# Gate logits with the gate as the stationary operand, shorter fills and a new plan in a fused expert, attention and expert layer

## The chip, the cores and the metric

The kernel runs on one core of a Trainium2 chip. The metric is the device time of one execution in microseconds. A core has TensorE (PE, with its weight loads listed as PEld), VectorE (DVE), ScalarE (ACT), GpSimd (POOL) and SyncE (SP, which issues most DMAs). TensorE reads SBUF and writes PSUM, which has eight banks of 128 partitions by 512 fp32 values. TensorE's clock is granted at one of two levels, 1.2 or 2.4 GHz; the profile gives the mean of a stretch as a share of the higher.

## What is computed

The input is 16 sequences of 512 tokens of width 128, in fp32. Three sublayers follow one another, called A, B and C in the kernel:

```python
x = x + 0.5 * ffn(layernorm(x), gate_w, gate_b, w1, b1, w2, b2)   # A
x = x + attn(layernorm(x), Wq, Wkv_down, Wk_up, Wv_up, Wo)        # B: 8 heads of 32
x = x + 0.5 * ffn(layernorm(x), gate_w, gate_b, w1, b1, w2, b2)   # C

def ffn(x, gate_w, gate_b, w1, b1, w2, b2):      # 8 experts, top 2, hidden 256
    logits = einsum('bsd,ed->bse', x, gate_w) + gate_b
    probs = softmax(logits)
    topk_vals, topk_idx = top_k(probs, 2)
    h = relu(einsum('bsd,edh->bseh', x, w1) + b1)
    expert_out = einsum('bseh,eho->bseo', h, w2) + b2
    return sum over the two chosen experts of expert_out * topk_vals
```

## The kernel before

**Tiling and stages.** A batch is one sequence: four tiles of 128 tokens. Stage B works on single batches. Stages A and C group batches into chunks (A: 1, 1, 2, 3, 3, 3, 3 batches; C: 3, 3, 3, 3, 2, 1, 1). One chunk of each stage, the first of A and the last of C, is dense: all experts for all tokens (`dh`, `dy`). The others are routed: GpSimd scatters normalized rows into expert order in DRAM with indirect DMAs (`scat`, L1091), the rows come back in quads of up to four tiles of 128 rows of one expert each (`xload`, `xg`), TensorE runs both expert layers (`h`, `y`) with weights fetched per tile (`wload`), results go to DRAM, and GpSimd gathers two rows for each token (`gat`, L1111) that VectorE combines (`comb`).

**Routing.** For each batch and each of A and C, GpSimd scales the rows (`scaled`, L1126), TensorE transposes them (`xTf`, L1674), ScalarE copies them to `xT_F` (L1256), and TensorE forms the gate logits (`logits`): four matmuls with the 128 tokens of a tile as stationary side and the gate's 8 columns as moving side, so that the tokens lie on PSUM's partitions. VectorE adds the gate bias (L1396), and once the chunk's batches are there runs the top-2 choice (`top1`, `top2`) and the ranks (`rank1`, `rank2`). The rank tables `same_expert` and `spread` (L1050 to L1054) are made by GpSimd at the kernel's start, ahead of everything in its order.

**Attention.** For each batch: layer norm on VectorE and ScalarE (`xnB`), transposes (`xT`), projections (`q`, `k`, `v`), and for each of two groups of four heads four steps of row maxima (`rmax`, four banks each: scores by TensorE, maximum by VectorE at L1541, exponentials and their sums by ScalarE at L1202), the split of the maxima and logarithms (`mrow`, L1772), four steps of scores (`s`: scores and maximum rows into four banks, exponentials by ScalarE at L1193), the product with V (`pv`, L1214 on ScalarE), and the output projection (`wo`). `by_rows` returns True for each group, so the branch with sums by additions on GpSimd (`add`, `sum`) has no step.

**What sets the order.** All work is cut into steps. `all_steps` gives each a wanted time from the constants at the head of the file (`PERIOD`, `WANTED`, the shifts), and `plan` simulates the engines with the costs of `PARTS` and the rings of buffers, taking on each engine the ready step with the smallest wanted time. The result is a fixed order for each engine and the PSUM bank of each step; it holds no times, since semaphores set those at run time. `GAP` is the least distance in the plan between two pairs of indirect DMAs.

**Fills.** `emptied_bank` (L1615) issues `TILES * KEEP[step]` transposes of the identity, whose result nobody reads, ahead of ten named steps: 12 times four ahead of the first batch's `xTf`, 10 times four ahead of attention batch 0's `xT`, and 12 times four at eight other steps together. `apart` (L1075) puts a memset of 900 columns of an unused tile ahead of any GpSimd step that directly follows a scatter or gather step.

```python
            def apart(at):
                if at.step in after_pair:
                    linked(pool.memset(pause[:], 0.0))
```

## Time and profile before

| | |
|---|---|
| median of 3 runs | 1193.15 us (1191.34 to 1196.9) |
| profiled execution, own time | 1193.1 us |
| its span | 1191.3 us |
| TensorE busy | 1139.1 us (96%) |
| ScalarE busy | 912.3 us (77%) |
| VectorE busy | 721.9 us (61%) |
| GpSimd busy | 714.4 us (60%) |
| mean granted clock | 0.97 |

Busy time is the union of an engine's instructions. A matmul in fp32 stands in the trace as two records (one for each pass over the operands), a transpose as one; their ends are modelled, so that TensorE can be shown busy where it waits between the matmuls of a group. The chain of waits is followed back from the last instruction to what released it. In a group of instructions the columns are busy time, mean duration of one, and the idle time of the engine just before them with what ended it.

### The profile page before, as it was taken

To read this page: it belongs to the slowest core of one execution; us is meant where nothing else is said; L and a number is where in the kernel's file an instruction comes from. 1 tells how busy PE (TensorE), PEld (TensorE's weight loads), DVE (VectorE), ACT (ScalarE), POOL (GpSimd) and SP (SyncE) were. 2 spreads that over 40 slices of the span, in tenths; PEclk is the share of its full clock that TensorE was granted. 3 is DMA by queue.
4 is the path that set the end of the run, shared out by engine and by line. 5 is a ranking of instruction groups with operands and counts; after the bars stand their busy time and mean duration, and the time that the engine had idled before them with its cause. 6 is when DMAs were issued, how large, how long until landed. Compare 5 with 4: busy or idle time off the path is not lost.

```text
span 1191.3 us, 26036 instructions
## 1 busy us (share of the span) xinstructions
PE 1139.1 (96%) x8278; PEld 759.2 (64%) x8278; DVE 721.9 (61%) x2254; ACT 912.3 (77%) x2255; POOL 714.4 (60%) x868
## 2 busy tenths in 40 slices
PE   7999998999999999999999999999999999999996
PEld 5677575676675557576666666666665456757675
DVE  4785568566785657375663676566657545647335
ACT  2348678678897989796898888888888887888431
POOL 3146568584848888028887653886701875268655
PEclk8998998999999999999999999999999889999988
DMA  8075573756645176656565636566732156548872
GB/s 287 1 251 167 176 224 110 243 159 204 203 136 149 47 227 210 177 149 183 178 210 154 181 123 183 161 206 196 211 107 63 41 159 178 148 148 249 257 257 73
DMA packets 159883, 202.07 MB, mean 170 GB/s; under 512 B 16938, under 2 KB 103426, under 8 KB 159747
## 3 DMA queue, kind: packets, MB, share of 16 engines
q1 hardware_dynamic: 144196, 168.90, 46.2%
q0 software_dynamic: 15360, 31.49, 9.1%
q8 instruction: 68, 1.11, 0.4%
q14 instruction: 67, 0.55, 0.2%
q10 hardware_dynamic: 192, 0.02, 0.0%
HBM read 152.50 MB, written 47.84 MB: 168 GB/s over the span
## 4 chain that ended last, share of the span: by engine, by line
PE 69%; POOL 10%; ACT 10%; issue 5%; DVE 3%; DMA 2%; SPq 0%; POOLq 0%; ACTq 0%; DVEq 0%
PE psum L1587 63%; ACT probs L1193 4%; ACT psum L1202 3%; POOL Y L1111 3%; POOL pause L1075 3%; PE psum L1707 2%; POOL slots_C L1091 2%; POOL slots_A L1091 2%; PE psum L1615 1%; PE psum L1772 1%; DVE neg_m L1541 1%; ACT hg L1239 1%; PE psum L1674 1%; DMA results_C<-ys 1%; ACT xnB L1158 1%
## 5 line engine op out<-in xcount | busy, mean ns | idle before, releaser
L1541 DVE TENSOR_REDUCE neg_m<-psum 128x1 f32<-128x512 f32 x512 | 317.6, 685 | 155.1 <-PE psum L1587 155.0
L1587 PE MATMUL psum<-nat 32*128 32x512 f32 x2048 | 364.4, 643 | 2.5 <-DVE ys L1521 1.4
L1202 ACT ACTIVATE psum<-psum,neg_m 128x512 f32<-128x512 f32 x512 | 341.6, 682 | 27.7 <-DVE neg_m L1541 26.9
L1193 ACT ACTIVATE probs<-psum 128x512 f32<-128x512 f32 x512 | 266.6, 630 | 43.2 <-PE psum L1587 41.6
L1587 PEld LDWEIGHTS psum<-nat 32*128 32x128 f32 x2048 | 130.6, 185 | 94.7 <-issue 24.3
L1075 POOL MEMSET pause<- 128x900 f32 x212 | 183.5, 866 | 0.1
L1587 PEld LDWEIGHTS psum<-xg_T,wt 128*128 128x128 f32 x1296 | 157.5, 195 | 40.2 <-ACT probs L1193 12.5
L1587 PE MATMUL psum<-xg_T,wt 128*128 128x128 f32 x1296 | 171.8, 283 | 5.3 <-DMA wt<-packed 3.5
L1587 PEld LDWEIGHTS psum<-wt,hg 128*128 128x128 f32 x1296 | 156.3, 196 | 31.6 <-ACT psum L1202 11.5
L1091 POOL DMA_INDIRECT slots_A<-xnA,posA x120 | 118.0, 983 | 95.0 <-DMA xs<-slots_A 44.9
L1587 PE MATMUL psum<-wt,hg 128*128 128x128 f32 x1296 | 166.7, 283 | 8.4 <-ACT psum L1202 3.7
L1111 POOL DMA_INDIRECT Y<-results_C,posC x120 | 115.8, 965 | 88.7 <-issue 68.3
L1091 POOL DMA_INDIRECT slots_C<-xnC,posC x120 | 117.8, 982 | 55.9 <-DVE posC L1490 21.2
L1111 POOL DMA_INDIRECT Y<-results_A,posA x120 | 116.0, 967 | 57.6 <-issue 29.6
L1587 PE MATMUL psum<-m_rows,heads_one 32*128 32x512 f32 x512 | 128.0, 765 | 0.0
L1239 ACT ACTIVATE hg<-psum 128x512 f32<-128x512 f32 (+1 forms) x168 | 97.1, 621 | 33.9 <-PE psum L1587 33.3
L1587 PE MATMUL psum<-probs,V 128*32 128x512 f32 x1024 | 117.3, 598 | 5.3 <-ACT probs L1193 4.9
L1521 DVE TENSOR_TENSOR ys<-psum,wt 128x512 f32<-128x512 f32 x84 | 57.0, 678 | 101.9 <-PE psum L1587 101.4
L1202 ACT ACTIVATION_READ_ACCUMULATOR psum<-psum,neg_m 128x1 f32 x512 | 116.4, 227 | 0.0
L1126 POOL TENSOR_SCALAR xnC<-X,rstdC,shiftC 128x128 f32<-128x128 f32 x64 | 28.8, 459 | 124.3 <-DVE shiftC L1373 124.1
L1587 PEld LDWEIGHTS psum<-probs,V 128*32 128x32 f32 x1024 | 31.4, 110 | 73.8 <-issue 59.7
L1214 ACT ACTIVATE o_n<-psum 128x512 f32<-128x512 f32 x32 | 19.1, 597 | 52.3 <-PE psum L1587 52.0
(192 smaller groups left out, 1424.5 us busy)
## 6 DMA issues: line engine op xcount, KB each, us to landing
wt<-packed SPq DMA_DIRECT2D x324, 320.0 KB, 4.1
xs<-slots_A SPq DMA_DIRECT2D x36, 256.0 KB, 4.6
results_A<-ys SPq DMA_DIRECT2D x36, 256.0 KB
xs<-slots_C SPq DMA_DIRECT2D x36, 256.0 KB, 5.3
results_C<-ys SPq DMA_DIRECT2D x36, 256.0 KB
X<-in_L_attn_x_dram SPq DMA_DIRECT2D x16, 256.0 KB, 8.3
out_dram<-X SPq DMA_DIRECT2D x16, 256.0 KB
packed<-probs SPq DMA_DIRECT2D x1, 2560.0 KB, 8.2
```

The costliest lines, as they stand in the source:

```text
L1075: linked(pool.memset(pause[:], 0.0))
L1091: pool.indirect_dma_start(out=slots[s][:], out_offset=bass.IndirectOffsetOnAxis(ap=pos[s, c % C_RING][:, k, t:t + 1], axis=0), in_=xn[s][: ...
L1111: pool.indirect_dma_start(out=Y[:, i % Y_RING, k, n, :], out_offset=None, in_=results[s, c][:], in_offset=bass.IndirectOffsetOnAxis(ap=pos ...
L1126: last = pool.tensor_scalar(xn[s][:, xn_place(s, b) + n, :], X[:, b % X_RING, n, :], rstd[s][:, n:n + 1], shift[s][:, n:n + 1], ALU.mult, ...
L1193: act.activation(probs[:, kt, j, :], at.banks()[j][:], ACT.Exp).then_inc(a_done, 1)
L1202: act.activation(at.banks()[j][:], at.banks()[j][:], ACT.Exp, bias=neg_m[:, g, n, j:j + 1], accum_out=sums[:, g, n, j:j + 1]).then_inc(S[" ...
L1214: act.activation(o_n[:, at.k, :], bank[:], ACT.Copy).then_inc(a_done, 1)
L1239: act.activation(hg[:, i % HG_RING, 0:n, :, :].rearrange("p n u t -> p (n u t)"), bank[:, 0:n * UNITS * P], ACT.Relu).then_inc(a_done, 1)
L1521: V_.tensor_tensor(ys[:, i % YS_RING, 0:len(tiles), :], bank[:, 0:len(tiles) * P].rearrange("p (i d) -> p i d", d=D), wt[:, first:first + ...
L1541: V_.tensor_reduce(neg_m[:, g, n, j:j + 1], at.banks()[j][:], AX.X, ALU.max, negate=True).then_inc(S["r_done"], 1)
L1587: return nc.tensor.matmul(dst, w, m, start=start, stop=stop)
L1707: last = nc.tensor.transpose(bank[:, tokens(n)], xs[:, i % XS_RING, n, :], ident[:])
```

## The change

Six things are edited.

1. Logits. The gate becomes the stationary side, padded with zeros to 32 columns, and a tile's 128 tokens the moving side. The four tiles of a batch write to four groups of 32 PSUM partitions, in one bank (step `lgT`, new). ScalarE copies the 128x128 block to `lg_T`, TensorE transposes it (what the step `logits` now is), and VectorE adds the bias, reading 8 of each 32 columns. `lg_T` has one copy, so the next `lgT` copy waits for the transpose.
2. `xT_F` is free again when the four matmuls are done, as before, now counted on ScalarE's semaphore.
3. The rank tables are made by GpSimd after it has scaled the first rows of A, and no longer ahead of them.
4. The pause is two linked memsets of 150 columns instead of one of 900.
5. `KEEP` and its transposes are removed.
6. The constants of the plan are new: all wanted times and shifts, a part of `PARTS`, and `GAP` 2.95 instead of 3.4.

GpSimd's `add` is cut into four pieces; there is no such step in either kernel.

```diff
-PERIOD, FIRST_B = 54.81, 448.4
+PERIOD, FIRST_B = 54.12, 487.87
...
-KEEP = {("B", 0, "xT", 0): 10, ("B", 2, "xT", 0): 2, ("B", 4, "mrow", 1): 2, ("B", 13, "mrow", 0): 1,
-        ("A", 0, "xTf", 0): 12, ("A", 6, "h", 0): 1, ("C", 8, "h", 4): 2, ("C", 11, "logits", 0): 1,
-        ("C", 10, "y", 1): 2, ("C", 12, "xTf", 0): 1}
-GAP = 3.4
+GAP = 2.95
...
-    "load": ((("SP", 0.48),), 4.0), "logits": ((("PE", 0.9), ("DVE", 0.15)), 0.0),
+    "load": ((("SP", 0.48),), 4.0), "lgT": ((("PE", 0.45), ("ACT", 0.28)), 0.0),
+    "logits": ((("PE", 0.17), ("DVE", 0.15)), 0.0),
...
-        gw_T, gate_bias = sb("gw_T", [P, EXPERTS]), sb("gate_bias", [P, EXPERTS])
+        gw_T, gate_bias = sb("gw_T", [P, P // TILES]), sb("gate_bias", [P, EXPERTS])
+        lg_T = sb("lg_T", [P, P])
...
-        pause = sb("pause", [P, 900])
+        pause = sb("pause", [P, 2, 150])
...
             def apart(at):
 
                 if at.step in after_pair:
-                    linked(pool.memset(pause[:], 0.0))
+                    for n in range(2):
+                        linked(pool.memset(pause[:, n, :], 0.0))
...
                 last.then_inc(S["rows_done"], 1)
+                if (s, b) == ("A", 0):
+                    rank_tables()
...
+            def lgT(at):
+
+                bank = a_bank(at)
+                i = lgT_order.index((at.stage, at.index))
+                if i:
+                    s0, b0 = lgT_order[i - 1]
                     act.wait_ge(d_full, counts["d_full", (s0, b0, "logits", 0)])
-                act.activation(xT_F[:, xTf_place(s, b), :], a_bank(at)[:], ACT.Copy).then_inc(a_done, 1)
+                act.activation(lg_T[:], bank[:, 0:P], ACT.Copy).then_inc(a_done, 1)
...
-                for _ in range(TILES * KEEP.get(at.step, 0) if not j else 0):
-                    nc.tensor.transpose(psum[bank][:, 0:P], ident[:], ident[:])
...
-            def logits(at):
+            def lgT(at):
                 bank = emptied_bank(at)
                 pe.wait_ge(setup_dve, 3)
                 pe.wait_ge(a_done, at.count("a_done", "xTf", 0))
                 i = xTf_place(at.stage, at.index)
+                rows = P // TILES
                 for n in range(TILES):
-                    last = pe_mm(bank[:, n * EXPERTS:(n + 1) * EXPERTS], xT_F[:, i, tokens(n)], gw_T[:])
-                last.then_inc(d_full, 1)
+                    last = pe_mm(bank[n * rows:(n + 1) * rows, 0:P], gw_T[:], xT_F[:, i, tokens(n)])
+                last.then_inc(a_full, 1)
+
+            def logits(at):
+                bank = emptied_bank(at)
+                pe.wait_ge(a_done, at.count("a_done", "lgT", 0))
+                nc.tensor.transpose(bank[:, 0:P], lg_T[:], ident[:]).then_inc(d_full, 1)
```

## Rows read from the trace of the kernel before

**Rows 1.** The page: busy times, the clock row, the chain by engine and line.

```profile
PE 1139.1 (96%) x8278; PEld 759.2 (64%) x8278; DVE 721.9 (61%) x2254; ACT 912.3 (77%) x2255; POOL 714.4 (60%) x868
...
PEclk8998998999999999999999999999999889999988
...
PE 69%; POOL 10%; ACT 10%; issue 5%; DVE 3%; DMA 2%; SPq 0%; POOLq 0%; ACTq 0%; DVEq 0%
PE psum L1587 63%; ACT probs L1193 4%; ACT psum L1202 3%; POOL Y L1111 3%; POOL pause L1075 3%; PE psum L1707 2%; POOL slots_C L1091 2%; POOL slots_A L1091 2%; PE psum L1615 1%; PE psum L1772 1%; DVE neg_m L1541 1%; ACT hg L1239 1%; PE psum L1674 1%; DMA results_C<-ys 1%; ACT xnB L1158 1%
```

**Rows 2.** TensorE's groups by form: count, then busy us, mean ns, idle before.

```profile
L1587 PE MATMUL psum<-nat 32*128 32x512 f32 x2048 | 364.4, 643 | 2.5 <-DVE ys L1521 1.4 <-ACT psum L1202 0.5 <-ACT nat L1269 0.4
...
L1587 PE MATMUL psum<-m_rows,heads_one 32*128 32x512 f32 x512 | 128.0, 765 | 0.0
L1587 PE MATMUL psum<-probs,V 128*32 128x512 f32 x1024 | 117.3, 598 | 5.3 <-ACT probs L1193 4.9 <-issue 0.3
L1707 PE MATMUL psum<-ident,xs 128*128 128x128 f32 x324 | 48.7, 279 | 0.0
L1587 PE MATMUL psum<-gw_T,xT_F 128*128 128x8 f32 x256 | 32.8, 254 | 2.7 <-ACT xT_F L1256 2.3 <-DVE gw_T L1315 0.3
...
L1615 PE MATMUL psum<-ident 128*128 128x128 f32 x136 | 21.1, 319 | 0.8 <-ACT psum L1202 0.8
```

**Rows 3.** Timeline of TensorE and ScalarE: start us, length us, operation, idle before.

```profile
185.86 4.27 PE L1587 MATMUL psum<-nat 32*128 32x512 f32 x16
...
1110.46 1.14 PE L1587 MATMUL psum<-nat 32*128 32x512 f32 x8
...
1111.77 2.05 PE L1587 MATMUL psum<-wt,hg 128*128 128x128 f32 x16
...
1119.75 3.64 PE L1587 MATMUL psum<-probs,V 128*32 128x512 f32 x32 [1.14 <-ACT probs L1193]
...
1123.32 2.05 PE L1587 MATMUL psum<-wt,hg 128*128 128x128 f32 x16
...
1129.08 0.38 ACT L1239 ACTIVATE hg<-psum 128x256 f32<-128x256 f32 x1
```

**Rows 4.** Windows: length, busy PE, PEld, DVE, ACT, POOL, granted clock, DMA, GB/s.

```profile
20.00:31.00 11.00, 11.00 (x29) 5.64 (x29) 7.39 (x43) 4.27 (x12) 2.94 (x7) 0.53 0.56 207
...
962.00:973.00 11.00, 11.00 (x44) 6.60 (x45) 3.55 (x14) 9.68 (x24) 8.47 (x12) 0.53 0.77 228
```

**Rows 5.** Windows with L1615 alone: length, PE and PEld busy, clock, DMA.

```profile
5.81:13.17 7.36, 7.36 (x48) 7.36 (x48) 1.00 1.08 313
...
68.50:71.40 2.90, 2.90 (x14) 2.90 (x15) 0.50 1.04 389
71.40:74.45 3.05, 3.05 (x28) 2.98 (x26) 0.95 1.02 383
```

**Rows 6.** Timeline of the start, and of attention batch 0's rows.

```profile
3.94 3.89 POOL L1050 TENSOR_SCALAR_AFFINE_SELECT same_expert<-same_expert 128x8 f32<-128x8 f32 x12
...
6.45 0.17 DVE L1373 TENSOR_SCALAR shiftA<-shiftA 128x4 f32<-128x4 f32 x1
...
9.74 1.75 POOL L1126 TENSOR_SCALAR xnA<-X,rstdA,shiftA 128x128 f32<-128x128 f32 x4
...
72.27 1.65 ACT L1158 ACTIVATE xnB<-X,shiftB,rstdB 128x128 f32<-128x128 f32 x4 [2.25 <-DVE shiftB L1373]
```

**Rows 7.** GpSimd's groups by form.

```profile
L1075 POOL MEMSET pause<- 128x900 f32 x212 | 183.5, 866 | 0.1
...
L1050 POOL TENSOR_SCALAR_AFFINE_SELECT same_expert<-same_expert 128x8 f32<-128x8 f32 x12 | 2.3, 192 | 1.6
...
L1037 POOL MEMSET ones<- 128x128 f32 x1 | 0.2, 202 | 0.0
```

**Rows 8.** Timeline of GpSimd's last gathers, first and last.

```profile
1143.49 0.99 POOL L1111 DMA_INDIRECT Y<-results_C,posC  x1 [7.84 <-issue]
...
1181.71 0.95 POOL L1111 DMA_INDIRECT Y<-results_C,posC  x1 [0.30 <-issue]
```

More of the change, by code:

```diff
@@ L148, in wanted_experts @@
             at[s, b, "load", 0] = t - 12.0
-        for n, name in enumerate(("norm", "scaled", "xTf", "logits")):
+        for n, name in enumerate(("norm", "scaled", "xTf", "lgT", "logits")):
             at[s, b, name, 0] = t + 2.0 * n
@@ L338, in all_steps @@
             steps[s, b, "xTf", 0].takes.append("xTf_dense" if c == DENSE[s] else "xTf")
-            after((s, b, "logits", 0), (s, b, "xTf", 0), (s, b - 1, "logits", 0))
+            after((s, b, "lgT", 0), (s, b, "xTf", 0), (s, b - 1, "lgT", 0))
+            steps[s, b, "lgT", 0].takes.append("lgT")
+            after((s, b, "logits", 0), (s, b, "lgT", 0), (s, b - 1, "logits", 0))
+            steps[s, b, "logits", 0].gives.append((0, "lgT"))
             if c == DENSE[s]:
@@ L342, in all_steps @@
             else:
-                steps[s, b, "logits", 0].gives.append((0, "xTf"))
+                steps[s, b, "lgT", 0].gives.append((0, "xTf"))
             if b == FIRST[c]:
-                after((s, b, "logits", 0), (s, c - 1, "gate", 0), (s, c - 1, "top2", 0))
+                after((s, b, "lgT", 0), (s, c - 1, "gate", 0), (s, c - 1, "top2", 0))
             after((s, c, "top1", 0), (s, b, "logits", 0))
@@ L740, in macaron_kernel @@
     xTf_order = list(xTf_turn)
+    lgT_order = [st[:2] for st in order["PE"] if st[2] == "lgT"]
     routed = [st[:2] for st in order["DVE"] if st[2] == "top1"]
     scaled_steps = [st for st in order["DVE"] if st[2] == "scaled"]
-    first_steps = order["PE"][:order["PE"].index(("A", 0, "logits", 0))]
+    first_steps = order["PE"][:order["PE"].index(("A", 0, "lgT", 0))]
     assert all(bank != GATE_BANK for step in first_steps for bank, _ in order["banks"][step])
@@ L1048, in _, with rank_tables @@
                                pattern=[[1, EXPERTS], [-1, EXPERTS]], channel_multiplier=0)
[L1049 to L1057 removed]
+            def rank_tables():
+                for t in range(T_MAX):
+                    linked(pool.affine_select(out=same_expert[:], in_=same_expert[:], compare_op=ALU.not_equal, fill=1.0,
+                                              base=-t * EXPERTS, pattern=[[-1, EXPERTS]], channel_multiplier=1))
+                pool.tensor_copy(spread[:, 0:EXPERTS], same_expert[:])
+                for t in range(T_MAX):
+                    last = pool.affine_select(out=spread[:, (t + 1) * EXPERTS:(t + 2) * EXPERTS], in_=same_expert[:],
+                                              compare_op=ALU.is_gt, fill=0.0, base=t * EXPERTS, pattern=[[0, EXPERTS]],
+                                              channel_multiplier=-1)
+                last.then_inc(consts_made, 1)
             def add(at):
@@ L1066, in add, with tokens @@
                     wait(pool, d_full, at.count("d_full", "sum", g, index))
-                pool.tensor_tensor(pairs[:, kt // 2, j, :], probs[:, kt - 1, j, :], probs[:, kt, j, :],
-                                   ALU.add).then_inc(S["p_added"], 1)
+                for n in range(TILES):
+                    last = pool.tensor_tensor(pairs[:, kt // 2, j, tokens(n)], probs[:, kt - 1, j, tokens(n)],
+                                              probs[:, kt, j, tokens(n)], ALU.add)
+                last.then_inc(S["p_added"], 1)
+            def tokens(n):
+                return slice(n * P, (n + 1) * P)
             after_pair = {step for old, step in zip(order["POOL"], order["POOL"][1:]) if old[2] in ("scat", "gat")}
@@ L1303, in _ @@
             chain = Chain(dve, link)
+            chain(V_.memset(gw_T[:], 0.0))
             V_.memset(M[:, 0:EXPERTS], 0.0)
```

61 lines of the change are left out of this document (27 added, 34 removed), and 4 rows, old and new, of the table PARTS.

## The prediction

> **What bounds the kernel now.** I read the page first: the busy shares and the clock row [rows 1]. The reader is to see TensorE at 96% busy and ScalarE at 77%, a granted clock that leaves the full level in few slices, and a chain of waits that is 69% TensorE, 10% GpSimd and 10% ScalarE. Taken at its word, that is a kernel bound by TensorE, and every microsecond taken from TensorE would be a microsecond of the whole.
>
> The second view, TensorE's groups by form, says to be careful [rows 2]. The score products (`psum<-nat`, with the maximum rows `m_rows`) are busy 364.4 + 128.0 = 492.4 us. There are 128 groups for the maxima (8 records each) and 128 for the scores (8 and 4). Where nothing holds them, a score group takes 1111.77 - 1110.46 = 1.31 us to the start of the next operation, and eight `nat` records alone 1.14 us [rows 3]. 128 x (1.31 + 1.14) = 314 us, so about 178 us of the 492 is TensorE waiting between the matmuls of a group for ScalarE to empty a bank; the stretch of 4.27 us for 16 records at full clock [rows 3] shows one. Busy TensorE is thus partly paced by ScalarE. I therefore take from the chain only the share that it gives TensorE, 0.69, for what is saved on TensorE in the middle of the kernel.
>
> The third view, windows around the places where the clock row dips [rows 4]: a stretch with clock c holds 2 x (1 - c) of its length at 1.2 GHz. There are ten such places (from 20, 68, 88, 191, 252, 563, 713, 931, 962 and 1133 us), about 65 us in all, so roughly 33 us of work time is lost to the lower level. Before each, TensorE either stood idle or was in paced score products.
>
> **The change part by part**, against the profiled execution's own 1193.1 us (the median of the runs is 1193.15, so nothing has to be shifted).
>
> *Logits.* Removed: 256 records of 8 columns, 32.8 us, 1.03 us for each of 32 batches [rows 2]; each loads 128 columns of weights for 8 columns of data. Added: four matmuls (eight records) with 32 columns of weights and 128 of data, in four column groups, and one transpose. The nearest row for the first is the product of probabilities and V, of the same weight shape but 512 columns: 1123.32 - 1119.75 = 3.57 us for eight rounds of four records [rows 3], 0.45 us a round. A quarter of the columns makes 0.11, two rounds 0.22 us: the lower bound. If the time is per instruction and not per column, 117.3 / 1024 = 0.115 us a record [rows 2] gives 0.92 us: the upper bound. I take 0.35, near the column bound, since the four records of a round run side by side in that row. The transpose costs 48.7 / 324 = 0.15 us [rows 2]. New cost 0.50 us (0.37 to 1.07), saved 0.53 x 32 = 17 us (from -1 to 21), times 0.69: **-12 us** (+1 to -15).
> The change of array shape shows no price of its own here: the full-width product starts at 1123.32, before the modelled end of the column-group one at 1123.39 [rows 3]. The Trainium skill (TensorEngine Tiling (Array Packing), section Key Properties) says that a change of tiling mode drains TensorE, which speaks against this edit; if two drains a batch cost as much as the 0.53 us saved, the sum would lose its 12 us.
> ScalarE gets 32 copies of 128 columns. A copy of 256 columns takes 0.38 us [rows 3], so at most 0.38 each; I take 0.28, 9 us, which at ScalarE's 10% of the chain is **+1 us** (0 to +9, if ScalarE is the pacer everywhere). Behind the new copy queue the score exponentials. VectorE's addition reads as many elements as before; the new wait of the transpose on that copy is covered by whatever TensorE does between, and costs some 0.3 + 0.3 us of routing latency where nothing is there: at the dense batches. The padding of the gate to 32 columns and its fill are at VectorE's start, ahead of the first rows' statistics, where it waits anyway.
>
> *Keep-warm transposes.* 136 records and 21.1 us go [rows 2]. 48 of them (7.36 us) fill the wait for the first rows, 40 (2.90 + 3.05 us) the wait for the rows of attention batch 0 [rows 5]. The other 48 are the rest, 21.1 - 13.3 = 7.8 us on TensorE's line, times 0.69: **-5 us** (0 to -8).
>
> *First rows ahead of the rank tables.* GpSimd spends 3.94 to 9.74 us on the tables and only then scales the first rows, until 11.49 [rows 6]; yet the fill holds TensorE until 13.17 [rows 5]. The tables are wanted only by the first routing step, late enough. The rows' shift is there at 6.62 us [rows 6], so rows at 8.4 and TensorE's first transposes of them at about 8.6: 4.6 us earlier. But the engine has then had no work. In [rows 5] the fill spent its first part on that. The cold places are 3.4 to 10.3 us long, so work that starts cold gives 1.7 to 5 us back. Net **-2 us** (-5 to +1).
>
> *Attention batch 0.* Its rows end at 72.27 + 1.65 = 73.92 [rows 6], the fill at 74.45, so 0.5 us is freed. But in [rows 5] the clock is at 0.50 in the first part of the fill and at 0.95 in the second: the fill brought it back. Without it the projections behind run cold for 3.4 to 7 us: 1.7 to 3.5 us lost. Net **+2 us** (-0.5 to +3).
> The Trainium skill (TensorE: Matmul & The Clock Gate, section Part 4: PE-mode transpose) says that transposes do not count as activity for the clock. By that the fills were worthless and this line is -0.5, the next one 0. The measured rise, with nothing but such transposes running since 68.5 us, says otherwise, and I go by it.
>
> *The clock elsewhere.* The 48 short fills of eight places go without anything in their stead. How many new falls this makes no row shows; at none, 0, at all eight with the mean cold length of 6.5 us, 8 x 3.3 = 26 us. I take one and a half: **+5 us**.
>
> *Short fills on GpSimd.* The pause (900 elements) takes 866 ns, 128 elements take 202 ns [rows 7]: 0.86 ns an element, so 150 take 221 ns. Two in line, with 0.13 us between (twelve linked selects of 192 ns leave 1.6 us idle before them [rows 7]), make 0.57 us: 0.29 less for each pair of indirect transfers, which come (1181.71 - 1.26 - 1143.49) / 11 = 3.36 us apart in the tail [rows 8] and would come 3.07 apart; over 212 pauses that is 62 us. GpSimd is not full, so most of it is idle time. On the chain stand Y 3, pause 3 and slots 2 + 2%, 10% or 119 us [rows 1]; 0.29 / 3.36 of it is 10 us at most. At least, the last 12 pairs, back to back from 1143.49 to 1182.7 [rows 8], which end after TensorE: 12 x 0.29 = 3.5 us. That needs TensorE to finish earlier too, which the other savings allow. I take **-6 us**. If the indirect transfers themselves set the spacing, 0. GpSimd's additions of probabilities, cut in four, do not occur: every group takes its sums by rows.
>
> *The new order.* New wanted times, costs and a gap of 2.95 instead of 3.4 reorder every engine. The trace of before cannot show it: nothing in the centre, 15 us either way.
>
> Sum: -12 + 1 - 5 - 2 + 2 + 5 - 6 = -17; 1193.1 - 17 = **1176 us**.
>
> **The rivals.**
> *Paced by ScalarE.* If the 178 us of waiting inside the score groups is the true bound, what TensorE saves turns into longer waits. Only the tail and the start are left, less ScalarE's copies at a third of their 9 us: 1193.1 - 3.5 - 2 + 3 = 1191. For it: ScalarE's 77% beside the waits; against: 69% of the chain.
> *More cold stretches: slower.* The order changes and nothing is left that fills a gap. Place: the score groups between 150 and 1120 us. Price 3.3 us a fall, against 22 us of savings without the clock term; slower than before from seven new falls on, and at twelve, 1193.1 - 22 + 40 = 1211. For it: five of the ten old falls came with TensorE recorded busy, two of them in [rows 4]. Against: the fills stood in eight places only.
> *The fills on GpSimd bring nothing*, the spacing staying at 3.36 us: the 6 us go, 1182.
> *A better order.* If it takes a tenth of the 178 us of waits, 1176 - 18 = 1158. For it: that much is there to take.
>
> **How the numbers follow.** Chances: the forecast (1165 to 1187) 0.45, useless fills on GpSimd 0.10, paced by ScalarE 0.15, more cold stretches 0.15, better order 0.15. The range from 1153 to 1200 takes in the better order, the pacing case and the mildest of the cold one. A measurement of this kernel tells 0.5%, 6 us, from no change. Faster: 0.45 + 0.10 + 0.15 and a third of the pacing case, 0.75; same: 0.10, slower: 0.15.
>
> **What would show it.** The logits' records: 256 of 128x128 data with 32 columns of weights, near 0.35 us a batch, and 32 transposes; busy TensorE down by some 38 us to about 1101. The pause pairs at 0.57 us and pairs of transfers 3.07 us apart in the tail. TensorE's first transposes of rows near 8.6 us. Cold stretches: ten to twelve, 65 to 80 us. I am wrong if the span falls far less than TensorE's busy time (pacing), if cold stretches exceed a dozen and a half, or if the waits inside the score groups change by more than 20 us either way (then the order decided).

## The result and the profile after

The changed kernel takes 1273.16 us (median of 4 runs, 1269.24 to 1276.56) where the kernel before takes 1195.03 beside it: a ratio of 1.0656, with a 95% interval from 1.0612 to 1.07. Forecast were 1176 us, in a range from 1153 to 1200. The sign was wrong, and the range missed by 73 us. The profiled run has a span of 1274.8 us.

Of the page of the changed kernel: busy times, the clock row, GpSimd's row, and the chain by engine.

```profile
PE 1173.5 (92%) x8174; PEld 754.0 (59%) x8174; DVE 703.1 (55%) x2255; ACT 919.7 (72%) x2287; POOL 629.6 (49%) x1084
...
POOL 3137378373667760005575547770016774276344
PEclk9979998999889899999999998999999989998988
...
PE 69%; ACT 12%; issue 6%; DVE 5%; POOL 2%; DMA 2%; another core or an unknown queue 2%; SPq 2%; DVEq 0%; ACTq 0%; POOLq 0%
```

Against [rows 1], TensorE is busy 34 us longer with 104 records fewer, and idle 101 us instead of 52. The mean clock fell from 0.97 to 0.95. GpSimd works 85 us less, and it has almost left the chain (2% instead of 10%). "Another core" cannot be meant literally, since there is only one. It is the label for a wait that ended with a semaphore increment more than 1.5 us after the end of any instruction that makes it, and it will turn out to be the most useful word on this page. "Issue" stands where no such increment is recorded at all. The two traces differ in that: this one holds 12,990 semaphore events, that of the kernel before 21,612, so busy and idle times can be compared between them, but the shares of "issue" and of "another core" cannot.

TensorE's groups by form in the changed kernel: count, then busy us, mean ns, idle before and what ended it.

```profile
L1611 PE MATMUL psum<-nat 32*128 32x512 f32 x2048 | 404.9, 666 | 8.7 <-issue 4.4 <-ACT psum L1216 1.8 <-ACT nat L1292 0.8
...
L1611 PE MATMUL psum<-wt,hg 128*128 128x128 f32 x1296 | 172.6, 289 | 21.0 <-issue 8.8 <-ACT hg L1253 7.5 <-DVE X L1489 2.4
L1611 PE MATMUL psum<-m_rows,heads_one 32*128 32x512 f32 x512 | 134.1, 782 | 0.0
...
L1611 PE MATMUL psum<-xT_F,gw_T 128*32 128x128 f32 x256 | 15.3, 301 | 6.2 <-ACT xT_F L1270 4.8 <-issue 1.2 <-DVE gw_T L1339 0.3
...
L1689 PE MATMUL psum<-ident,xnB 128*128 128x128 f32 x64 | 10.4, 287 | 11.7 <-ACT xnB L1172 11.7
...
L1712 PE MATMUL psum<-ident,lg_T 128*128 128x128 f32 x32 | 9.9, 310 | 2.8 <-ACT lg_T L1279 1.4 <-DVE ys L1545 1.3
```

The score products stand at 404.9 + 134.1 = 539 us against 492.4 [rows 2]: 47 us more, with no record added. The logits cost 15.3 + 9.9 = 25.2 us instead of 32.8. The changed operations are visible and small; most of the loss lies in waits inside and before work that was not touched.

### The profile page after: what moved, and what is told of

The parts are those of the page before. It is cut to its first block, busy times and chain, and to the rows that moved or that the text cites. A ratio compares the mean times of both kernels' runs of the same rounds, so it can differ in the third digit from the quotient of the medians.

```text
span 1274.8 us, 26148 instructions
## 1 busy us (share of the span) xinstructions
PE 1173.5 (92%) x8174; PEld 754.0 (59%) x8174; DVE 703.1 (55%) x2255; ACT 919.7 (72%) x2287; POOL 629.6 (49%) x1084
## 4 chain that ended last, share of the span: by engine, by line
PE 69%; ACT 12%; issue 6%; DVE 5%; POOL 2%; DMA 2%; another core or an unknown queue 2%; SPq 2%; DVEq 0%; ACTq 0%; POOLq 0%
PE psum L1611 64%; ACT psum L1216 5%; ACT probs L1207 4%; PE psum L1735 3%; DVE neg_m L1565 2%; DMA wt<-packed 1%; PE psum L1800 1%; POOL slots_A L1103 1%; PE psum L1696 1%; ACT hg L1253 1%; DMA X<-in_L_attn_x_dram 1%; DVE X L1530 1%; ACT xnB L1172 1%; POOL Y L1123 1%
## 5 line engine op out<-in xcount | busy, mean ns | idle before, releaser
L1611 PE MATMUL psum<-nat 32*128 32x512 f32 x2048 | 404.9, 666 | 8.7 <-issue 4.4
L1611 PEld LDWEIGHTS psum<-nat 32*128 32x128 f32 x2048 | 149.9, 191 | 114.2 <-issue 54.4
L1611 PEld LDWEIGHTS psum<-xg_T,wt 128*128 128x128 f32 x1296 | 161.6, 197 | 52.6 <-issue 35.2
L1611 PE MATMUL psum<-wt,hg 128*128 128x128 f32 x1296 | 172.6, 289 | 21.0 <-issue 8.8
L1611 PE MATMUL psum<-xg_T,wt 128*128 128x128 f32 x1296 | 178.6, 286 | 12.5 <-DMA wt<-packed 7.7
L1611 PEld LDWEIGHTS psum<-wt,hg 128*128 128x128 f32 x1296 | 160.7, 201 | 49.7 <-issue 20.7
L1611 PE MATMUL psum<-m_rows,heads_one 32*128 32x512 f32 x512 | 134.1, 782 | 0.0
L1611 PE MATMUL psum<-probs,V 128*32 128x512 f32 x1024 | 121.5, 610 | 7.5 <-ACT probs L1207 6.0
L1545 DVE TENSOR_TENSOR ys<-psum,wt 128x512 f32<-128x512 f32 (+1 forms) x84 | 56.2, 669 | 126.6 <-PE psum L1611 78.3
L1087 POOL MEMSET pause<- 128x150 f32 x428 | 99.3, 232 | 12.5
```

Source lines behind the costliest of these rows:

```text
L1087: linked(pool.memset(pause[:, n, :], 0.0))
L1545: V_.tensor_tensor(ys[:, i % YS_RING, 0:len(tiles), :], bank[:, 0:len(tiles) * P].rearrange("p (i d) -> p i d", d=D), wt[:, first:first + ...
L1611: return nc.tensor.matmul(dst, w, m, start=start, stop=stop)
```

## The experiments

The runs were made in five sets, and in each the kernel before was timed on the same chip: 1190.7, 1191.9, 1194.1, 1192.5 and 1191.0 us on the chips numbered 6, 4, 15, 8 and 13. The chip of the first measurement above is not on record. The chip of a run is named below, because it matters. "Distance" is the time from one pair of indirect transfers to the next while GpSimd has nothing else to do.

### The parts alone, in the order of before (chip 6)

**b_nokeep**: without the keep-warm transposes.

```diff
-KEEP = {("B", 0, "xT", 0): 10, ...
+KEEP = {}
```

> The kernel before without any of its 136 keep-warm transposes, order unchanged. My prediction's steps give: -5 (short ones), +2 (attention batch 0), +5 (other cold stretches), and the start no earlier: 1195, range 1186 to 1215. If these transposes do not count for the clock, 1186 to 1190. Theory P needs here a good part of the loss: 1215 or more.

Measured 1193.77 us, ratio 1.003 [1.0005, 1.0055], so +3 us. The prediction's three terms for these transposes (-5 on TensorE, +2 at attention batch 0, +5 for the clock) sum to +2.

**b_rows_first**: the rank tables behind the first rows, and without the 48 transposes that fill the wait for them; the other 88 stay.

```diff
-        ("A", 0, "xTf", 0): 12, ("A", 6, "h", 0): 1, ("C", 8, "h", 4): 2, ("C", 11, "logits", 0): 1,
+        ("A", 6, "h", 0): 1, ("C", 8, "h", 4): 2, ("C", 11, "logits", 0): 1,
...
+                if (s, b) == ("A", 0):
+                    rank_tables()
```

> The kernel before with the rank tables behind the first rows and without the 48 keep-warm transposes ahead of them, the other 88 kept. My prediction's step: TensorE's first transposes of rows at 8.6 us and not 13.2, 1.7 to 5 us given back by a cold start, in sum -2 us: 1188 to 1194. A rival: the whole later order is paced by DMAs and weights, and nothing moves: 1192 to 1196 with TensorE idle later in the first 70 us.

Measured 1188.98 us, ratio 0.9993 [0.9969, 1.0017]: -1 us, not told apart from nothing.

**b_short**: two linked fills of 150 columns.

```diff
-        pause = sb("pause", [P, 900])
+        pause = sb("pause", [P, 2, 150])
-                    linked(pool.memset(pause[:], 0.0))
+                    for n in range(2):
+                        linked(pool.memset(pause[:, n, :], 0.0))
```

> The kernel before with two linked fills of 150 columns in the place of one of 900, order unchanged. Theory S: 1225 to 1250 us, with unexplained waits of TensorE of some 20 to 25 us that before does not have. Theory P, and my prediction's own step: 1186 to 1193, the tail shorter by 3.5 us.

Measured 1182.62 us, ratio 0.9936 [0.9909, 0.9963]: -8 us. On this chip three parts of the change come within 2 us of their forecast sums.

**a_long**: the changed kernel with the 900-column fill of before.

```diff
-        pause = sb("pause", [P, 2, 150])
+        pause = sb("pause", [P, 900])
```

> The changed kernel with one fill of 900 columns in the place of two of 150; every engine's order is the same. Theory S (the short fills are the cause: with pairs of indirect transfers 3.0 us apart other engines are held up, up to 2.6 us at a time, with no cause in the records): 1200 to 1225 us, TensorE's unexplained waits (25 us in 30 places after the change) under 3 us, pairs 3.36 us apart. Theory P (the new plan and the missing keep-warm transposes are the cause): 1265 to 1280, as it also slows GpSimd by 61 us in all.

Measured 1237.64 us, ratio 1.0391 [1.0331, 1.045]. All of the change but the fill (new order, new logits, first rows first, no keep-warm transposes) costs 47 us beside the kernel before, and yet the time is 36 us below that of the changed kernel. So the short fills, which gave 8 us in one order, seemed to take 36 in the other; but the 36 compares two chips.

### Logits alone, order alone, fill in one piece (chip 4)

**after_again**: the changed kernel unchanged.

> The changed kernel itself, on the chip of this set, for a trace with its semaphore events whole: in the first one about 40% of these records are missing, and so waits of 1 to 3 us of ScalarE and TensorE stand there without a cause. 1265 to 1280 us; if the waits have causes now, they name what the short fills collide with in this order.

1281.32 us, ratio 1.0744 [1.07, 1.0787].

**a_one**: one fill of 500 columns, which lasts as long as the two of 150.

```diff
+        pause = sb("pause", [P, 500])
+                    linked(pool.memset(pause[:], 0.0))
```

> The changed kernel with one fill of 500 columns, which lasts as long as the two linked ones of 150 (0.52 us). Theory D (distance: pairs of indirect transfers 3.0 us apart are too dense for this order): as the changed kernel, 1265 to 1280. Theory L (the two linked fills and their semaphore traffic harm): as with the one long fill, 1230 to 1245.

1286.63 us, ratio 1.0745 [1.0687, 1.0802]. It is not the link between two fills: one unlinked fill of the same length is no faster.

**c_logits**: the new logits put into the orders of before. The other steps of each engine keep their order; the copy and the transpose are inserted where the plan says that their inputs are there, and VectorE adds the bias a few places later.

```diff
+    split_logits(order)
+                    last = pe_mm(bank[n * rows:(n + 1) * rows, 0:P], gw_T[:], xT_F[:, i, tokens(n)])
```

> The kernel before with only the new logits (gate stationary in four column groups, copy by ScalarE, one transpose); the old order of each engine is kept, with the copy and the transpose put in where their inputs are there by the plan, and the bias addition a few places later on VectorE. My prediction's step: -11 us, 1178 to 1184 (bounds 1175 to 1200). Theory M (each change between full array and column groups drains TensorE and costs what is saved): 1188 to 1200.

1206.71 us, ratio 1.0116 [1.0073, 1.0158]: 15 us slower, where 11 us faster would have been the sum of the parts. Two of TensorE's groups in c_logits:

```profile
L1622 PE MATMUL psum<-xT_F,gw_T 128*32 128x128 f32 x256 | 13.9, 288 | 2.6 <-ACT xT_F L1282 1.9 <-issue 0.5 <-DVE gw_T L1349 0.3
...
L1725 PE MATMUL psum<-ident,lg_T 128*128 128x128 f32 x32 | 10.3, 322 | 15.2 <-ACT lg_T L1289 11.0 <-ACT probs L1219 2.0 <-ACT psum L1228 1.4
```

The transposes find their copy not ready: 15.2 us of idle TensorE before 32 of them, 11.0 of it for `lg_T`. The copy queues behind exponentials, as the prediction said (in the longest of these waits it starts 1.5 to 2.1 us after its products end), but the price was put at nothing outside the dense batches. The price belongs to this insertion, though: in the changed kernel, whose order was drawn with the new step in it, 2.8 us of idle time stand before the same 32 transposes, and 0.1 to 0.6 with the longer fills (a_long, a_long2, a_700).

**b_newplan**: the code of before, with its logits and its long fill, under the new constants and costs and without keep-warm transposes (+3 us in b_nokeep).

```diff
-GAP = 3.4
+GAP = 2.95
+KEEP = {}
```

(and the other constants of the change)

> The kernel before with only the new constants and costs of the plan (no keep-warm transposes, long fill, old logits, tables first). The plan's own model ends 43 us later with these than with the old ones. Theory O (order: the old constants were fitted so closely that another draw of the order loses on the chip about twice what its model says, through paced score groups and cold stretches): 1240 to 1275. If the order is harmless and the new logits step is what costs: 1195 to 1230.

1287.22 us, ratio 1.077 [1.071, 1.083]. An order can cost some 90 us with nothing else of the change beside it. It is not the changed kernel's order: drawn from the same constants, but with the old logits, the plan ends at 1219 us by its own model, where that of the changed kernel ends at 1188. Groups of TensorE in b_newplan:

```profile
L1705 PE MATMUL psum<-ident,xs 128*128 128x128 f32 x324 | 51.0, 289 | 10.9 <-DMA xs<-slots_A 8.0 <-DMA xs<-slots_C 1.4 <-ACT psum L1200 1.2
...
L1672 PE MATMUL psum<-ident,xnC 128*128 128x128 f32 x64 | 12.0, 319 | 13.2 <-POOL xnC L1124 13.2
...
L1672 PE MATMUL psum<-ident,xnA 128*128 128x128 f32 x64 | 10.9, 297 | 11.6 <-POOL xnA L1124 10.6 <-ACT psum L1200 0.7 <-issue 0.2
```

All three wait for GpSimd: for rows that it scales, and for the slots that its scatters fill. Together they hold 35.7 us of idle time; in the kernel before the same three groups hold 3.6. This order was drawn for a distance of 2.95 us and ran with 3.36. Following the planner's own model with the orders held fixed and only the distance changed, b_newplan ends at 1219 with 2.95 and at 1279 with 3.36. The same for the changed kernel's order: 1188 with 2.95, 1194 with 3.02, 1220 with 3.21, 1244 with 3.36 (a_long measured 1238). For the order of before: 1173 with 2.95, 1174 with 3.36. That is the first answer: the old order has room on GpSimd and hardly asks for the distance; the new one is drawn to the edge of it. By the model it needs the short fills. But they did not help it.

### The same kernels side by side (chip 15)

**after3**, **a_long2** and **b_short2** are the changed kernel, a_long and b_short again, with nothing edited.

> The changed kernel once more, unchanged, beside the same kernel with the long fill (next run) on one chip. So far the long fill stood at 1237.6 us and the short fills at 1273 and 1281, but in separate calls. Theory fill (the shorter distance between indirect transfers costs time in this order): this one again near 1275, 30 to 40 us above the next. Theory chip or call: both within 10 us of each other.

> The changed kernel with one fill of 900 columns instead of two of 150, the same as a_long. Theory fill: 1238 again, a third of the added time of the change gone. Theory chip or call: within 10 us of after3, whatever that gives.

> The kernel before with the two short fills alone, the same as b_short. Theory that the fills help where the order was drawn with room for them: 1182 to 1185 again, ratio 0.99 to 0.996. Theory that b_short owed its gain to its call: 1191 or more.

after3 took 1273.37 us (ratio 1.0647 [1.0598, 1.0695]), a_long2 1233.69 (1.0328 [1.0282, 1.0374]). So the short fills cost the new order 40 us, both timed on one chip. And b_short2, the very kernel that had taken 1182.62 us on chip 6, took **1286.58** here (ratio 1.0768 [1.0698, 1.0838]; runs 1280.97 to 1295.0), with the kernel before at 1194.1 beside it. Both theories on b_short2 were too tame: what gives 8 us on one chip costs 92 on another.

The two traces hold the same instructions in the same order, so the place can be read off. b_short on chip 6, timeline: start us, length us, operation, idle before.

```profile
216.25 2.05 PE L1588 MATMUL psum<-wt,hg 128*128 128x128 f32 x16
...
218.14 1.95 PE L1588 MATMUL psum<-xg_T,wt 128*128 128x128 f32 x16
...
218.34 0.69 DVE L1522 TENSOR_TENSOR ys<-psum,wt 128x512 f32<-128x512 f32 x1 [0.56 <-PE psum L1588]
```

The same instructions in b_short2, on chip 15:

```profile
221.98 2.05 PE L1588 MATMUL psum<-wt,hg 128*128 128x128 f32 x16
...
223.87 1.95 PE L1588 MATMUL psum<-xg_T,wt 128*128 128x128 f32 x16
...
226.54 0.96 POOL L1112 DMA_INDIRECT Y<-results_A,posA  x1 [0.27 <-issue]
...
227.16 0.69 DVE L1522 TENSOR_TENSOR ys<-psum,wt 128x512 f32<-128x512 f32 x1 [3.62 <-remote]
...
227.96 0.60 ACT L1240 ACTIVATE hg<-psum 128x512 f32<-128x512 f32 x1 [2.22 <-PE psum L1708]
...
230.22 2.11 PE L1588 MATMUL psum<-wt,hg 128*128 128x128 f32 x14 [3.53 <-ACT hg L1240]
```

On chip 6 VectorE starts 0.04 us after the products end (218.30). On chip 15 they end at 224.03 and VectorE starts 3.13 us later, with nothing before it. ScalarE's `hg` starts 2.1 us after its own products ended (225.82). TensorE in turn waits 3.53 us. GpSimd goes on in its rhythm meanwhile. I call this a **late release**: the work is done, the waiting engine is free, and it starts 2 to 3 us later. Laying the starts of TensorE's instructions in the two traces over each other, 93 of the 106 us of difference arise where pairs of transfers follow closely on one another, or within 3 us behind such a stretch (814 us of the span), and 13 in the rest (471 us).

The trace says one thing more. VectorE waits here for a semaphore that TensorE increments; the increment is recorded at 218.31 on chip 6 and at 227.14 on chip 15, 0.02 us before VectorE starts in both. So VectorE is not slow to see it: the increment itself comes 3.1 us after the modelled end of the products. The same holds for the increment that ScalarE's `hg` waits for (227.94). Over all 84 additions of VectorE into `ys`, counted from the end of their products or of VectorE's own work before, whichever is later: in b_short none starts over 0.3 us late, in b_short2 eleven start over 1 us late (3.7 at most), and all eleven have their increment recorded within 0.1 us before they start.

The group of `ys`, without its twelve smaller instructions, shows it for a whole kernel. VectorE's `ys<-psum,wt` (72 instructions) in b_short, then in b_short2, a_long2 and after3:

```profile
L1522 DVE TENSOR_TENSOR ys<-psum,wt 128x512 f32<-128x512 f32 x72 | 49.5, 688 | 98.9 <-PE psum L1588 98.8
```

```profile
L1522 DVE TENSOR_TENSOR ys<-psum,wt 128x512 f32<-128x512 f32 x72 | 49.6, 689 | 138.3 <-PE psum L1588 99.6 <-remote 36.4 <-issue 2.0
```

```profile
L1544 DVE TENSOR_TENSOR ys<-psum,wt 128x512 f32<-128x512 f32 x72 | 49.4, 688 | 69.1 <-PE psum L1610 51.2 <-issue 17.6
```

```profile
L1545 DVE TENSOR_TENSOR ys<-psum,wt 128x512 f32<-128x512 f32 x72 | 49.6, 689 | 121.9 <-PE psum L1611 69.9 <-remote 31.5 <-issue 20.4
```

"Remote" is the label of "another core" in this view; it stands there with the short fills and not with the long one. In b_short2, 31 waits of over 1 us on VectorE and ScalarE end so, and none in b_short; TensorE has no wait with this label, but 16.0 us of waits without a recorded cause. In the first trace of the changed kernel it is 24.3 us, in after_again 25.0, in a_one 33.3; in the `ys` of b_newplan and c_logits, on the same chip 4, none. So b_newplan's loss and the changed kernel's loss, though alike in size, are two different ones. The score products grow with the late releases too, with no change of order:

```profile
L1588 PE MATMUL psum<-nat 32*128 32x512 f32 x2048 | 364.6, 644 | 0.8 <-ACT nat L1270 0.4 <-ACT psum L1203 0.2
```

```profile
L1588 PE MATMUL psum<-nat 32*128 32x512 f32 x2048 | 399.7, 664 | 10.6 <-issue 2.8 <-DVE ys L1522 2.6 <-ACT probs L1194 2.5
```

The first is b_short, the second b_short2: 35 us more (and 137.2 instead of 128.5 us for the maximum rows).

**b_nudge**: the kernel before with one planner constant moved by 0.01 us, to see what any other order costs.

```diff
-GAP = 3.4
+GAP = 3.39
```

> The kernel before with one constant of its planner moved by 0.01 us (the distance of indirect transfers, 3.39 instead of 3.40). No operation is added or removed; the planner draws another order (708 of TensorE's 929 steps keep their relative order, the first difference is step 211), which by the planner's own model ends at 1190.8 instead of 1175.5 us. Theory A (the planner's model tells what an order costs): 15 us slower, 1205 to 1210. Theory B (any order but the given one runs 50 to 80 us behind its model, as that of the changed kernel does): 1240 to 1270. Theory C (the order does not matter): 1191 to 1195.

1212.55 us, ratio 1.0132 [1.0077, 1.0186]: +18 us, by its model +15. Theory A comes close (its range ended at 1210). Here an order costs about what the model says, and a change of constants that looks like nothing redraws a quarter of TensorE's steps.

### Distance or rhythm (chip 8)

**after4**: the changed kernel unchanged.

> The changed kernel unchanged, once more. The two short fills alone, in the order of before, gave 1182.6 us on one chip and 1286.6 us on another, where before itself gave 1190.7 and 1194.1. Theory (late releases during dense indirect transfers are a property of some chips): on a chip like the first the changed kernel takes 1195 to 1215, on one like the second 1273 again. Rival (the new order itself costs the 80 us): 1270 or more on any chip.

1278.94 us, ratio 1.0746 [1.0667, 1.0825].

**b_700** and **b_even**: one fill of 700 columns after each pair; one of 150 after each single transfer.

```diff
-        pause = sb("pause", [P, 900])
+        pause = sb("pause", [P, 700])
```

```diff
                 for k in range(2):
+                    if k:
+                        linked(pool.memset(pause[:, 1, :], 0.0))
                     pool.indirect_dma_start(...)
```

> The kernel before with one fill of 700 columns instead of 900: pairs of indirect transfers about 3.19 us apart, between 3.36 (before) and 3.01 (short fills). On a chip where short fills cost time: if the cost grows evenly with the distance taken away, half of the 92 us, 1235 to 1245; if there is a distance below which it begins, either 1190 or 1280. On a chip where they cost none: 1187.

> The kernel before with one 150-column fill after every single transfer in place of one 900-column fill after every pair: the same pace as with the two short fills (a pair in about 3.0 us), but evenly spaced, 1.5 us each instead of 1.26 and 1.75. On a chip where short fills cost time: theory pace (it is the number of transfers in a time that counts): 1280 again; theory distance within or after the pair: near 1190. On a chip where they cost none: 1183.

b_700 took 1181.34 us, ratio 0.9899 [0.984, 0.9959]; b_even 1376.69, ratio 1.1513 [1.1435, 1.159]. The timelines of GpSimd, b_700 first:

```profile
305.61 0.96 POOL L1111 DMA_INDIRECT Y<-results_A,posA  x1 [0.27 <-POOL pause L1075]
306.87 0.95 POOL L1111 DMA_INDIRECT Y<-results_A,posA  x1 [0.31 <-issue]
307.81 0.71 POOL L1075 MEMSET pause<- 128x700 f32 x1
308.79 0.96 POOL L1111 DMA_INDIRECT Y<-results_A,posA  x1 [0.27 <-POOL pause L1075]
```

```profile
335.70 0.96 POOL L1115 DMA_INDIRECT Y<-results_A,posA  x1 [0.27 <-issue]
336.66 0.24 POOL L1075 MEMSET pause<- 128x150 f32 x1
337.17 0.96 POOL L1115 DMA_INDIRECT Y<-results_A,posA  x1 [0.27 <-issue]
338.13 0.24 POOL L1114 MEMSET pause<- 128x150 f32 x1
338.64 0.96 POOL L1115 DMA_INDIRECT Y<-results_A,posA  x1 [0.27 <-issue]
```

And `ys` in b_700, then in b_even:

```profile
L1521 DVE TENSOR_TENSOR ys<-psum,wt 128x512 f32<-128x512 f32 x72 | 49.6, 688 | 97.3 <-PE psum L1587 77.4 <-issue 18.9 <-DVE at_slot L1419 0.9
```

```profile
L1525 DVE TENSOR_TENSOR ys<-psum,wt 128x512 f32<-128x512 f32 x72 | 49.6, 688 | 172.5 <-PE psum L1591 100.3 <-remote 72.0
```

At 3.21 us from pair to pair no addition into `ys` starts over 1 us late (three of 84 by 0.3 to 0.9 us), and the gain, 11 us, is no smaller than that of the short fills on chip 6. At 2.94 us (two times 1.47) they hold twice the time that they hold with the short fills (72.0 against 36.4), and the kernel loses 184 us. The theory on distance inside or after the pair falls: wider room inside the pair did not help. Pace is what b_even and b_short2 share, but pace alone would have given 1280, not 1377. So 0.07 us more of pace, or the even spacing, or both, doubled the cost. No run here parts these.

### The distance of 700 columns in the new order (chip 13)

**a_700**: the changed kernel, its order kept, with the 700-column fill. **a_plan**: the same with constants of its own and `GAP = 3.22`, searched against the planner's model for the distance that the fill gives, and with the old costs apart from the logits'. **b_600**: the kernel before with 600 columns.

```diff
-        pause = sb("pause", [P, 2, 150])
+        pause = sb("pause", [P, 700])
```

(a_700; b_600 has 600 in place of before's 900)

```diff
-GAP = 2.95
+GAP = 3.22
```

(a_plan, with 700 columns and its other constants)

> The changed kernel in its own order with one fill of 700 columns in place of the two of 150: 3.21 us between pairs, where the order was drawn for 2.95. Following the planner's model with the order fixed and 3.21 put in for the distance, the end moves from 1188 to 1220 (with 3.36, the long fill, to 1244, where 1234 and 1238 were measured). Theory (no late releases at 3.21, but GpSimd paces): 1210 to 1220, 55 to 65 below the changed kernel. Rival (late releases stay, since they belong to the new order): 1270.

> The changed kernel's edits (new logits, first rows first, no keep-warm transposes) with one fill of 700 columns (pairs of transfers measured 3.21 us apart in b_700, 1181.3 us) and with an order of its own, drawn for that distance: the planner's distance is 3.22 and its other constants were searched against its own model, which ends this order at 1169.1 us (before: 1175.5, measured 1190 to 1195; the changed kernel: 1188.1). Theory (an order costs what its model says, as long as the model's distance is what the fill gives and the distance stays above the one where late releases begin): 1169 + 6 to 19 = 1175 to 1188. Rival (the new logits cost time in any order, as they did in c_logits, +14): 1195 or more. Rival (any order but the given one runs 50 us behind its model): 1220 or more.

> The kernel before with one fill of 600 columns: pairs about 3.12 us apart, between b_700 (3.21 us, 1181) and the short fills (3.01 us, 1286 on such a chip). If the late releases begin below 3.12: 1180 to 1183. If above: 1200 to 1260.

a_700 took 1211.36 us, ratio 1.018 [1.0135, 1.0225]; a_plan 1192.67, ratio 1.0017 [0.9994, 1.0039]; b_600 1182.83, ratio 0.9929 [0.9903, 0.9954].

From 1273 to 1281 down to 1211: at 3.21 us the changed kernel takes 62 to 70 us less. The two were not timed on one chip, and chip 13 is of the kind on which no late release was seen at any distance. That the longer fill would do the same on the other kind is not shown in this order; it is likely, since b_700 has no late release of over 1 us on chip 8, and since a_long and a_long2 agree within 4 us across the two kinds. Shown on one chip are the 40 us between after3 and a_long2. Part of what is left is GpSimd, by the chain of a_long2, and then of a_700, by engine:

```profile
PE 38%; POOL 34%; issue 14%; DVE 5%; DMA 4%; ACT 3%; SPq 1%; POOLq 0%; DVEq 0%; ACTq 0%
```

```profile
PE 51%; POOL 22%; issue 9%; ACT 7%; DVE 4%; DMA 4%; SPq 2%; POOLq 0%; DVEq 0%; ACTq 0%
```

In the kernel before GpSimd has 10% of it [rows 1]. At 3.36 us it has 34% of the chain, at 3.21 it has 22%.

a_plan missed its range (1175 to 1188) by 5 us and lies 24 us above its model, where before lies 15 to 20 above. With the new logits, the first rows first, no keep-warm transposes, and an order drawn for them and for 3.22 us, the kernel is as fast as before, and 10 us slower than b_600 beside it, which has nothing but a shorter fill. The rival of a_plan that the new logits cost time in any order (1195 or more) is not excluded: the gain of 8 to 11 us that the fill brings elsewhere is missing.

b_600 cannot narrow the onset. Chip 13 is like chip 6 in a respect that goes with the late releases: its traces hold about 21,700 semaphore events, those from the chips 4, 15 and 8 from 12,700 to 14,600, with and without late releases. All late releases were seen on chips of the second kind, and so was the first trace of the changed kernel (12,990 events). Whether the recording takes part in them is open: every run has its span and clock from such a record, so no time here was taken without one.

The version that beats both is **b_700**: the kernel before with a fill of 700 columns, 0.9899 of its time on a chip on which the short fills cost. b_600 gained 0.7% and was run on the other kind only.

## Why the prediction was wrong

The step that failed is **"The new order: nothing in the centre, 15 us either way"**, together with the one ahead of it, **"Short fills on GpSimd: -6, at least -3.5; if the indirect transfers themselves set the spacing, 0"**.

*Short fills.* The pair came 3.01 us apart, forecast 3.07, and two fills last 0.52, forecast 0.57. The price was about right on chip 6 (-8 for -6). But the bound was drawn on one side only, at zero: the spacing had no worse end. On three of the four numbered chips on which it ran, the shorter distance goes with late releases on VectorE and ScalarE, for which TensorE then waits. In the old order it cost 92 us (chip 15). In the new one it cost 40 us against the long fill on one chip, and 62 to 70 against 700 columns on another (1273 to 1281 against 1211). [Rows 8] showed the distance, and nothing in the trace of before could show what lies below it. The untried length of a wait that looks like pure waste deserves a bound on the slow side too.

*The new order.* Nothing in the trace of before prices an order, but the diff did: `GAP` from 3.4 to 2.95 says that the new order counts on the distance. Its own model ends 12.6 us later than that of before, and every 0.1 us by which the real distance is longer adds some 14 (1194 at 3.02, 1220 at 3.21). What is left at 3.21 us is +20 (a_700), of which 1211 - 1193 = 18 us goes when the order is redrawn (a_plan). "15 us either way" was too narrow even for this order (+20, and +47 with the long fill), and by a factor of six for the order of b_newplan (+95).

*Logits.* That TensorE's own work shrinks was right, its size was off. The four matmuls take 15.3 / 32 = 0.48 us a batch (forecast 0.35) and the transpose 0.31 (forecast 0.15), so 7.6 us come off TensorE's busy time, not 17. The transposes' price was read from a group that runs many in line, where their lengths overlap; single, one takes 310 ns, its own length. And the added chain from TensorE over ScalarE back to TensorE costs waits where the order leaves it no room: c_logits is 15 us slower where -11 was due. What it costs in the changed kernel's own order no run shows by itself. Before the 256 records of c_logits stand 2.6 us of idle time, 0.5 of them without a cause, so no pause shows ahead of them; the loss shown is in the 15.2 us of waits before the transposes. By the Trainium skill (TensorEngine Tiling (Array Packing), section Key Properties) each change of tiling mode drains TensorE; no run here separates that from the 0.26 us by which a batch lies above the column bound of 0.22.

*Keep-warm transposes, attention batch 0, the clock elsewhere.* Close in sum, +2 forecast and +3 in b_nokeep, but partly by luck. Behind the place of the fill b_nokeep works at half clock from 75.20 to 86.6 us, some 5.7 us lost where 1.7 to 3.5 were expected. Elsewhere no falls were added: leaving out the one at the very end, it has six half-clock stretches (51 us), the kernel before ten (65 us), so the +5 for the clock is not borne out. In the changed kernel the place itself went as follows. Timeline of TensorE:

```profile
61.48 0.60 PE L1696 MATMUL psum<-ident,xnA 128*128 128x128 f32 x4
71.36 1.09 PE L1689 MATMUL psum<-ident,xnB 128*128 128x128 f32 x4 [9.28 <-ACT xnB L1172]
```

An idle stretch of 9.28 us replaces the fill. The granted clock is at half from 65.5 us, in the middle of it, to 79.2: 7.8 us of work at half clock, about 4 us lost, where +2 was forecast. In the whole kernel half-clock stretches rose from ten (some 65 us) to 21 (122 us). That is past the "dozen and a half" set as the mark of error, but it is no cause: b_short and b_short2 are one program, and the clock is 0.975 in one and 0.940 in the other. With the late releases come idle times of TensorE and more half-clock stretches: 26 (150 us) in b_short2, 8 (55 us) in b_short.

*First rows.* Right: rows at 8.45 us (forecast 8.4), TensorE's transposes of them at 8.50 (8.6).

```profile
6.70 1.75 POOL L1138 TENSOR_SCALAR xnA<-X,rstdA,shiftA 128x128 f32<-128x128 f32 x4 [2.73 <-DVE shiftA L1397]
...
8.50 1.12 PE L1696 MATMUL psum<-ident,xnA 128*128 128x128 f32 x4 [2.68 <-POOL xnA L1138]
```

The start is cold, as forecast, though the granted clock in [rows 5] does not show it: it reads 1.00 over the first 20 us, before and after. The lengths do. These four transposes take 1.12 us, where behind the fill of before they take 0.60, and the six products behind them 5.8 us instead of 2.8: some 3.5 us of the 4.8 us gained are given back. b_rows_first shows -1 us for the forecast -2, within its noise.

*The rivals.* "More cold stretches: slower" had the right sign and a wrong mechanism; its price of 3.3 us a fall, for 11 new falls, gives 1193.1 - 22 + 36 = 1207, 66 us short. "Paced by ScalarE" is not borne out as the cause: it allowed for 1191, and ScalarE's share of the chain went from 10 to 12% only. TensorE's busy time was to fall to 1101 us; it rose to 1173.5, and at 3.21 us (a_700) it is 1126.2. Of the signs set beforehand, one misleads: the score products grew by 47 us, more than the 20 that were to mean that the order decided. b_short2 shows 44 us more than b_short in the same groups (536.9 against 493.1) in one and the same order, so late releases can do it alone; in a_700, in the new order at 3.21 us, the groups stand at 499.0. No rival had GpSimd's distance as a danger, though [rows 7] and the chain in [rows 1] pointed at it as something that the kernel before pays for on purpose.

*What stays open.* What the changed kernel takes on a chip like 6 or 13: it was timed four times, and all three numbered chips are of the other kind, as is, by its 12,990 events, the chip of the first trace. By a_700 and b_short an estimate is 1211 less up to 26 us (its model from 3.21 to 3.02), 1185 to 1211. At which distance between 3.01 and 3.21 us the late releases begin, whether spacing within the pair adds to them, why the increments come late, and what makes the chips differ was not settled.

## What to carry to other kernels

A fill or wait that looks like waste may hold down a rate that harms other engines. Give its removal a slow side, shorten it in steps (900, 700, 600 columns) rather than at once, and time it on more than one chip: here less than half of the shortening (3.36 to 3.21 us, not 3.01) brought 11 us on a chip of the kind on which the whole of it cost 92. A static order is tied to the constants that it was drawn for; when a cost changes in the machine or in the plan, follow the old order with the new cost first, and see whether it has room. And lay two traces of the same program over each other when their times differ: the first waits that differ show where to look, and the semaphore's increment, beside the end of the work and the start of the waiter, shows which of the two is late.

## What the runs showed of the hardware

- One kernel, b_short, took 1182.6 us on one chip and 1286.6 on another, while the kernel before differed by 0.3% between them. With pairs of indirect transfers 3.01 us apart, 11 to 14 of VectorE's 84 additions into `ys` start 1.0 to 3.7 us after the work that they wait for has ended, on the chips 4, 15 and 8; with 3.21 us (chip 8) or 3.36 us (chips 4 and 15) none is over 0.9 us late, and on the chips 6 and 13 none over 0.3 us at any distance that was run.
- What is late is the semaphore's increment: in the seven traces with a distance of 3.01 us and less on the chips 4, 15, 8 and that of the first trace, 85 of 86 such starts have it recorded within 0.1 us before them (11 of 11 in b_short2).
- Such waits are labelled "remote" in the trace, or have no recorded cause. VectorE's `ys` holds 24 to 36 us of "remote" waits at 3.01 us, 72 at 2.94 us, none at 3.12 us and above.
- A transpose of 128 columns that stands alone takes 310 to 323 ns of TensorE; in a line of many the same work comes to 150 ns each. Four matmuls of 128 columns in four column groups take 0.43 to 0.48 us.
